# Linear attention: the reciprocals of the denominators spread by one matmul a group instead of two

## The chip, the cores and the metric

The kernel runs on one core of one Trainium2 chip. The metric is the device time of one execution in microseconds (us); lower is better. Engines are named as in the profile: PE is TensorE's matmul and PEld its weight load, DVE is VectorE, ACT is ScalarE, POOL is GpSimd, and SP is SyncE, whose queue issues most of the transfers.

## The reference, cut to what matters

The reference is a decoder layer over x of 2 x 2048 x 512 values in f32: linear attention, then attention to 154 keys, then a mixture of experts. Only the first part matters here:

```python
q_proj = _elu1(einsum('bhnd,hdf->bhnf', q, proj_matrix))   # 16 heads, 128 features
k_proj = _elu1(einsum('bhnd,hdf->bhnf', k, proj_matrix))
kv   = einsum('bhnf,bhnd->bhfd', k_proj, v)
attn = einsum('bhnf,bhfd->bhnd', q_proj, kv)
z    = 1.0 / (einsum('bhnf,bhf->bhn', q_proj, k_proj.sum(axis=2)) + 1e-08)
x    = x + (attn * z[..., None]) heads side by side @ w_out + b_out
```

Each token has one denominator for each of 16 heads, and each of the 32 values of a head is multiplied by the reciprocal of that one denominator.

## The kernel before

Four stages follow one another, each in a block that all engines enter together: `project` (queries, keys, values, and the sums over the keys), `attend_linear`, `attend_cross` and `experts`. The change touches the first two.

Where more precision is wanted than PE's fp32r format keeps, a number is held in two parts: HI, the value rounded to fp32r, and LO, the rest. A product takes several matmuls over these parts.

In `project`, `ks_out(b)` (L552) puts the sums of the keys of one batch into `ks_w`. It has one matrix of 128 x 32 for each head. It is zero but for one column, the number of the head's group, g. Four copies on DVE of 128 x 4 values do that for 16 heads.

`attend_linear` works on 8 blocks of 512 tokens. The 16 heads stand in G = 4 groups of 4; head j of a group has partitions 32j to 32j+31. In `attend_group` (L1176, L1182) the matmuls with `ks_w` add up over the groups into `p_den`: row 32j+g is the denominator of head j of group g. ACT copies the bank to `den[:, 0]` and adds 1e-8 (L960), DVE takes the reciprocal in two halves of 256 columns (L1049), ACT rounds each half to HI (L965), POOL subtracts it to get LO (L924), and PE spreads: for each group a 0/1 matrix `spread[:, g]` copies row 32j+g to the 32 rows of head j, once for HI and once for LO, into one PSUM bank (`spread_out`, L1191). DVE multiplies the numerators by that bank (`normalise`, L1054). ACT and POOL split the product for the output projection (L971, L936).

Every engine runs through the same 8 slots for a block, and in each slot PE works on three blocks: heads of the block ahead, projection and layer norm of this one, and the queries XQ of the next attention for the one behind:

```python
    2: [("R", 0), ("R", 1), ("R", 2), ("R", 3), ("XQ", 2, 0, 12)],
    3: [("ND", 0), ("O", 0, 0, 12)],
```

R is `spread_out`, XQ is `queries` (L1226, 12 matmuls), O is `out_proj` (L1204), T is the transposes (L1213), ND is `attend_group`. Slot 0 holds XQ 0 and slot 1 XQ 1 of the block behind. R, XQ, O and T share three PSUM banks in the order in which they come, so each waits until the job three before it was read: in slot 2, R 2 waits for the read of XQ 1, R 3 for that of R 0, and XQ 2 for that of R 1. DVE reads them in its own order: in slot 2 it is `query(i-1, 1)` (L1091), `normalise` 0, a head (L1086), `normalise` 1 and 2, a head, `normalise` 3. The first query needs ACT's half of it before (L989).

The constants come in three DMAs on SP's queue, counted by `const_in`: `spread`, `bq` and `bias`. One for `x` follows.

Of the kernel before, what the change touches and what calls it, by code (L numbers as in the profile page):

```python
# [18 lines left out]
F32 = mybir.dt.float32  # L19
# [3 lines left out]
ACT = mybir.ActivationFunctionType  # L23
AX = mybir.AxisListType

P = 128
# [6 lines left out]
H = 16  # L33
# [41 lines left out]
def constants():  # L75

    ident = np.eye(P, dtype=np.float32)
    quad = np.arange(P) // HD
    key = np.arange(P) % HD
    mask = (quad[:, None] == np.arange(HG)).astype(np.float32)  # L80
    mask_keys = mask * (key < KREM)[:, None]

    spread = np.zeros((P, G, P), np.float32)
    for g in range(G):
        for p in range(P):
            spread[32 * quad[p] + g, g, p] = 1

    pick = (np.arange(P)[:, None] % HD == np.arange(E)).astype(np.float32)
    lower = np.zeros((P, E, E), np.float32)
    for e in range(E):  # L90
        lower[:, e, :e] = 1
    small = np.concatenate([mask, mask_keys], 1)
    return {
        "ident": ident, "small": small, "spread": spread.reshape(P, -1), "lower": lower.reshape(P, -1), "pick": pick,
    }


# [92 lines left out]
def project(nc, a, NBLK, BLK, x_blk, q_dram, ident, f_w, k3, q_in, q_out, kv_w, ks_w, w_kv, first_heads, half,  # L190
# [81 lines left out]
    with ExitStack() as ctx:  # L272
# [36 lines left out]
        def bank_of(key):  # L309
            return pj[POS[key] % BANKS]  # L310
# [18 lines left out]
        with nc.Block() as block:  # L329
# [169 lines left out]
            def _(dve):  # L499
# [46 lines left out]
                def ks_out(b):  # L546
                    if b == 0:
                        dve.wait_ge(zero_set, 2)
                    dve.wait_ge(filled, POS[(b, "KS")] + 1)
                    flat = ks_w[:, b].rearrange("p h d -> p (h d)")  # L550
                    for j in range(HG):
                        last = nc.vector.tensor_copy(flat[:, j * HD:(H - HG + j) * HD + G:HG * HD + 1],  # L552
                                                     bank_of((b, "KS"))[:, 2 * j:2 * (H - HG + j) + 1:2 * HG])
                        last.then_inc(*((dve_read, 1) if j == HG - 1 else (sums_set, 1)))

                def bend(key):

# [205 lines left out]
def attend_linear(nc, a, NBLK, BLK, x_blk, q_dram, x1_dram, xq_dram, ident, f_w, q3, q_in, q_out, xq_out, kv_w, ks_w, qp,  # L763
# [35 lines left out]
    with ExitStack() as ctx:  # L799
# [10 lines left out]
        u_ln = sb("u_ln", [P, 2, C, TB], F32R)  # L810
        spread = sb("spread", [P, G, P], F32R)
        rec = sb("rec", [P, 2, TB], F32R)
        bias = sb("bias", [P, D])
        x = sb("x", [P, TT, D])
        xn = sb("xn", [P, 2, D])
# [2 lines left out]

        bq = sb("bq", [P, C])
        tiny = sb("tiny", [P, 1])  # L820
        stats = sb("stats", [P, TT, 6])
        mv = sb("mv", [P, TT, 2])
        rstd = sb("rstd", [P, TT])
# [37 lines left out]
        with nc.Block() as block:  # L861
            @block.sync
            def _(sp):
                def load_q(b, g):

                    sp.wait_ge(h_full, H * (b - 2) + HG * (g + 1))
                    if b == NBLK - 1 and g == 0:
                        for landed in q_out:
                            sp.wait_ge(landed, 16 * Q_DMAS * NBLK)
                    load_group(sp, q_dram, b, g, q3, q_in[g])  # L870

                def query_out(m, g):
                    sp.wait_ge(xq_taken, G * m + g + 1)
                    sp.dma_start(xq_dram[m].rearrange("s p n -> p s n")[:, :, g * TB:(g + 1) * TB],
                                 xq[:, g % 2].bitcast(F32)).then_inc(xq_out[g % 2], 16)

                sp.dma_start(spread_raw.rearrange("p g n -> p (g n)"), a["spread"]).then_inc(const_in, 16)
                sp.dma_start(bq[:], a["bqT"]).then_inc(const_in, 16)
                sp.dma_start(bias[:], a["b_out"].broadcast_to([P, D])).then_inc(const_in, 16)
                sp.dma_start(x[:], x_blk[0]).then_inc(x_in, 16)  # L880

                def slot(i, s, ahead, now, behind):
                    if behind and s in (1, 2, 3, 7):
                        query_out(i - 1, (1, 2, 3, 7).index(s))
                    if i >= 0 and i + 2 < NBLK and s in (2, 4, 6, 7):
                        load_q(i + 2, (2, 4, 6, 7).index(s))
                    if now and s == 6:
                        sp.wait_ge(o_taken, TT * (i + 1))
                        sp.dma_start(x1_dram[i], x[:].rearrange("p t d -> p (t d)")).then_inc(x1_out, 16)
                    if now and s == 7 and i + 1 < NBLK:  # L890
                        sp.wait_ge(x1_out, 16 * (i + 1))
                        sp.wait_ge(xn_set, TT * (i + 1))
                        sp.dma_start(x[:], x_blk[i + 1]).then_inc(x_in, 16)
                    if i == NBLK - 1 and s == 0:

                        sp.wait_ge(h_full, H * (NBLK - 1))
                        sp.dma_start(first.ctx[:], a["ctxT"][0].rearrange("(c p) n -> p c n", p=P))\
                            .then_inc(first.sems["ctx_in"], 16)
                        sp.dma_start(first.bk[:], a["bkT"]).then_inc(first.sems["ctx_in"], 16)
                    if i == 0 and s == 7:  # L900
                        sp.wait_ge(wo_lo, 1)
                        sp.wait_ge(wq_lo, 1)
                        for n, name in enumerate(("WkT", "WvT", "WoT")):
                            sp.dma_start(staged(stage, n), a[name].rearrange("(c p) n -> p c n", p=P)).then_inc(next_in, 16)

                turns(slot)
                sp.wait_ge(next_in, 48)
                sp.wait_ge(scaled, 1)
                sp.wait_ge(x1_out, 16 * NBLK)

            @block.gpsimd
            def _(pool):
                nc.gpsimd.memset(tiny[:], 1e-8).then_inc(tiny_set, 1)
                pool.wait_ge(tiny_set, 1)
                pool.wait_ge(const_in, 48)
                def add_bias(i, t):
                    if t == 0:
                        pool.wait_ge(x_in, 16 * (i + 1))
                    nc.gpsimd.tensor_tensor(x[:, t], x[:, t], bias[:], ALU.add).then_inc(xb_set, 1)

                def reciprocal_low(i, n):
                    cols = slice(n * TB // 2, (n + 1) * TB // 2)
                    pool.wait_ge(rec_hi, 2 * i + n + 1)
                    nc.gpsimd.tensor_tensor(rec[:, LO, cols], den[:, 1, cols], rec[:, HI, cols].bitcast(F32),  # L924
                                            ALU.subtract).then_inc(rec_set, 1)

                for i in range(NBLK):
                    if i == 0:
                        pool.wait_ge(spread_set, 1)
                    reciprocal_low(i, 0)  # L930
                    reciprocal_low(i, 1)
                    add_bias(i, 0)
                    add_bias(i, 1)
                    for g in range(G):
                        pool.wait_ge(norm_hi, G * i + g + 1)
                        nc.gpsimd.tensor_tensor(u_att[:, LO, g], num[:, g], u_att[:, HI, g].bitcast(F32), ALU.subtract)\  # L936
                            .then_inc(norm_lo, 1)
                    add_bias(i, 2)
                    add_bias(i, 3)
                    for t in range(TT):  # L940
                        pool.wait_ge(aggr_set, 2 * (TT * i + t + 1))
                        nc.gpsimd.tensor_tensor(rstd[:, t:t + 1], mv[:, t, 1:2], half[:, 0:1], ALU.pow)\
                            .then_inc(rstd_set, 1)

            @block.scalar
            def _(act):
# [15 lines left out]
                def reciprocal_high(i, n):  # L962
                    cols = slice(n * TB // 2, (n + 1) * TB // 2)
                    act.wait_ge(recip_set, 2 * i + n + 1)
                    nc.scalar.copy(rec[:, HI, cols], den[:, 1, cols]).then_inc(rec_hi, 1)  # L965

                def normalised(i, g):
                    if g == 0:
# [13 lines left out]

                def query(m, g):
                    if m == 0 and g == 0:
                        act.wait_ge(const_in, 48)
                    if m or g >= 2:
                        act.wait_ge(xq_out[g % 2], 16 * (2 * m + g // 2))
                    act.wait_ge(xq_full, G * m + g + 1)
# [56 lines left out]
            def _(dve):  # L1045
# [49 lines left out]
                def slot(i, s, ahead, now, behind):  # L1095
                    first, second = [(lambda h=h: head(i + 1, h)) if ahead else (lambda: None)
                                     for h in range(PER * s, PER * (s + 1))]
                    if i == -1 and s == SLOTS - 1:
                        dve.wait_ge(const_in, 48)
                        nc.vector.tensor_copy(spread[:], spread_raw).then_inc(spread_set, 1)  # L1100
                    if s == 1 and now:
                        reciprocal(i, 1)
# [50 lines left out]
            def _(pe):  # L1153
# [32 lines left out]
                def spread_out(i, g):  # L1186
                    bank_free((i, "R", g))
                    if g == 0:
                        pe.wait_ge(rec_set, 2 * (i + 1))
                    for s in (HI, LO):  # L1190
                        mm = nc.tensor.matmul(bank_of(i, "R", g)[:], spread[:, g], rec[:, s], start=(s == HI),  # L1191
                                              stop=(s == LO))
                    mm.then_inc(r_full, 1)

                def out_proj(i, t, lo, hi):
                    if lo == 0:
# [1481 lines left out]
```

## Time and profile before

| | |
|---|---|
| median of 3 runs | 2379.21 us (2376.5 to 2381.13) |
| the profiled execution | 2380.94 us, of which the span of the instructions is 2379.2 us |
| mean granted clock of TensorE | 0.983 of full speed |
| linear stage | about 417 to 743 us of the span |
| PE busy, whole span | 2278.0 us (96%) |

The page gives sums over all stages. Whether a matmul less is worth its time is to be read from the stage it stands in: there the timeline tells what PE waits for, right behind that matmul.

### The profile page before, as it was taken

The page shows a single profiled execution, that of the slowest core. Times are in us where ns is not written, and L with a number is a line of the kernel's source. Part 1 is how long each engine was busy: PE and PEld are TensorE (multiplying, and loading weights), DVE is VectorE, ACT ScalarE, POOL GpSimd, SP SyncE. Part 2 cuts the span into 40 slices and gives each one's busy share as a digit, 9 for nine tenths or more (in the row PEclk, how much of TensorE's full clock was granted, in tenths as well). Part 3 has the DMA queues.
Part 4 walks back from the last instruction along what each step waited for, and adds up shares of the span by engine and source line. Part 5 has one row for each costly group of instructions (what it writes and reads, how often), then busy time and mean ns, then how long its engine had stood idle before and what let it go on. Part 6 is the DMA issues. An engine that isn't in the chain of part 4 may idle for free.

```text
span 2379.2 us, 34267 instructions
## 1 busy us (share of the span) xinstructions
PE 2278.0 (96%) x12200; PEld 1775.7 (75%) x12200; DVE 1390.5 (58%) x2258; ACT 1158.5 (49%) x2745; POOL 838.9 (35%) x820
## 2 busy tenths in 40 slices
PE   7999999899998899998799999999999999999998
PEld 6888886566666566665588878888788887888887
DVE  5555456777774668777644466444664445644444
ACT  3555566767663767774544444333343333433332
POOL 1444345333341245545677762111111111111111
PEclk9999999999999899999899999999999999999999
DMA  7655546666646457784656546454345543464442
GB/s 209 161 146 128 134 107 157 210 187 195 177 142 181 102 145 188 185 225 138 217 174 212 177 141 214 171 177 142 129 153 201 177 142 125 136 215 139 140 139 77
DMA packets 140218, 387.46 MB, mean 163 GB/s; under 512 B 15920, under 2 KB 38064, under 8 KB 123440
## 3 DMA queue, kind: packets, MB, share of 16 engines
q1 hardware_dynamic: 139760, 384.77, 53.9%
q8 instruction: 98, 1.61, 0.3%
q10 hardware_dynamic: 288, 0.49, 0.1%
q14 instruction: 72, 0.59, 0.1%
HBM read 254.00 MB, written 104.07 MB: 151 GB/s over the span
## 4 chain that ended last, share of the span: by engine, by line
PE 51%; DVE 1%; issue 0%; ACT 0%; DVEq 0%
PE ex_pg L2593 32%; PE ex_pd L2609 18%; DVE ex_xb L2410 0%; PE ex_pd L2559 0%; PE ex_pd L2570 0%; DVE ex_up L2430 0%; DVE ex_acc L2447 0%; ACT ex_xb L2260 0%; DVE stage L2406 0%; DVE ex_ht L2439 0%; DVE ex_lg L2348 0%; DVE ex_rank L2382 0%; DVE ex_gt L2379 0%; DVE ex_rank L2380 0%; DVE ex_g L2423 0%
## 5 line engine op out<-in xcount | busy, mean ns | idle before, releaser
L2593 PE MATMUL ex_pg<-ex_xb,first_wg 128*128 128x512 f32 x3360 | 821.5, 391 | 12.0 <-DVE ex_up L2430 7.0
L2593 PEld LDWEIGHTS ex_pg<-ex_xb,first_wg 128*128 128x128 f32 x3360 | 632.0, 189 | 153.0 <-issue 15.7
L2609 PE MATMUL ex_pd<-ex_wd,ex_ht 128*128 128x512 f32 x1920 | 486.4, 389 | 2.9 <-issue 2.6
L2609 PEld LDWEIGHTS ex_pd<-ex_wd,ex_ht 128*128 128x128 f32 x1920 | 360.0, 188 | 79.1 <-issue 4.5
L2447 DVE SCALAR_TENSOR_TENSOR ex_acc<-ex_pd,ex_share,ex_acc 128x512 f32<-128x512 f32 x320 | 239.7, 749 | 302.4 <-PE ex_pd L2609 302.2
L2267 ACT COPY ex_m<-ex_pg 128x512 f32<-128x512 f32 x240 | 141.1, 588 | 383.5 <-PE ex_pg L2593 383.4
L2211 POOL TENSOR_TENSOR ex_h<-ex_g,ex_up 128x512 f32<-128x512 f32 x80 | 103.3, 1292 | 553.3 <-issue 458.2
L1590 ACT ACTIVATE cr_prob<-cr_s_bank,cr_top 128x154 f32<-128x154 f32 x512 | 194.7, 401 | 89.3 <-DVE cr_top L1700 86.6
L422 POOL TENSOR_TENSOR pr_ks_sum<-pr_ks_sum,pr_kp 128x512 f32<-128x512 f32 x128 | 165.2, 1291 | 161.6 <-DVE pr_kp L570 150.0
L2271 ACT ACTIVATE ex_g<-ex_g 128x512 f32<-128x512 f32 x160 | 101.3, 633 | 238.0 <-DVE ex_g L2423 165.5
L2203 POOL TENSOR_TENSOR ex_wd<-stage,ex_wd 128x512 fp32r<-128x512 f32 x80 | 105.8, 1343 | 260.1 <-ACT ex_wd L2248 260.1
L2278 ACT CAST ex_ht<-ex_h 128x512 fp32r<-128x512 f32 x160 | 99.4, 622 | 133.1 <-POOL ex_h L2211 133.0
L570 DVE SCALAR_TENSOR_TENSOR pr_kp<-pr_pk,pr_kp 128x512 f32<-128x512 f32 x128 | 88.5, 691 | 104.1 <-ACT pr_kp L475 103.4
L1700 DVE TENSOR_REDUCE cr_top<-cr_s_bank 128x3 f32<-128x462 f32 x192 | 110.4, 578 | 59.3 <-PE cr_s_bank L1865 59.2
L1865 PEld LDWEIGHTS cr_s_bank<-cr_k_w,cr_q 96*128 96x128 f32 x512 | 74.1, 199 | 77.1 <-issue 37.2
L2416 DVE TENSOR_TENSOR ex_g<-ex_pg,ex_m 128x512 f32<-128x512 f32 x80 | 55.3, 691 | 130.1 <-PE ex_pg L2593 124.9
L2439 DVE TENSOR_TENSOR ex_ht<-ex_h,ex_ht 128x512 fp32r<-128x512 f32 x160 | 122.2, 764 | 0.1
L1865 PE MATMUL cr_s_bank<-cr_k_w,cr_q 96*128 96x154 f32 x512 | 98.5, 302 | 20.1 <-DMA cr_q<-xq_scratch 11.9
L1590 ACT ACTIVATION_READ_ACCUMULATOR cr_prob<-cr_s_bank,cr_top 128x1 f32 x512 | 110.1, 215 | 0.0
L1927 PE MATMUL cr_bank<-cr_wo,cr_u 128*128 128x512 f32 x384 | 103.4, 407 | 4.0 <-DVE cr_x L1729 4.0
L1086 DVE SCALAR_TENSOR_TENSOR qp<-li_h_bank,qp 128x512 f32<-128x512 f32 x112 | 75.2, 681 | 46.7 <-ACT qp L1006 46.0
L473 ACT ACTIVATE pr_kp<-pr_pk 128x512 f32<-128x512 f32 x124 | 73.2, 590 | 52.8 <-PE pr_pk L702 52.8
(222 smaller groups left out, 3588.9 us busy)
## 6 DMA issues: line engine op xcount, KB each, us to landing
first_wg<-w_scratch SPq DMA_DIRECT2D x60, 1024.0 KB, 5.1
first_wg<-w_scratch SPq DMA_DIRECT2D x60, 768.0 KB, 4.3
w_scratch<-first_wg SPq DMA_DIRECT2D x20, 1792.0 KB, 6.8
stage<-in_units SPq DMA_DIRECT2D x60, 512.0 KB, 6.9
qk<-pr_kq SPq DMA_DIRECT2D x192, 128.0 KB, 2.4
qk<-q_scratch SPq DMA_DIRECT2D x96, 256.0 KB, 4.7
cr_q<-xq_scratch SPq DMA_DIRECT2D x96, 256.0 KB, 8.0
q_scratch<-pr_kq SPq DMA_DIRECT2D x128, 128.0 KB, 2.3
```

The source lines that it names most:

```text
L422: nc.gpsimd.tensor_tensor(part, part, slot(step), ALU.add).then_inc(ks_step, 1)
L1590: last = nc.scalar.activation(prob[:, n % 2, t, j, 0:KEYS], s_bank[(MU * n + v) % SBANKS][:, at * KEYS:(at + 1) * KEYS], ACT.Exp, bias=top ...
L1700: nc.vector.tensor_reduce(dst.rearrange("p t j -> p (t j)") if t == t_end else dst[:, :, 0], src, AX.X, ALU.max, negate=True).then_inc(top ...
L1865: mm = nc.tensor.matmul(s_bank[at % SBANKS][:, k * KEYS:(k + 1) * KEYS], q3[:, n % QRING, j, t * P:(t + 1) * P], k_w[:, n // G // BLK, j, ...
L1927: mm = nc.tensor.matmul(bank_of("O", m)[:], u[:, s, g, tile_cols(m)], wo[:, w, g], start=(n == 0), stop=(n == 3 * G - 1))
L2203: nc.gpsimd.tensor_tensor(wd[:, n % 2, LO, cols], d_raw[:, cols], wd[:, n % 2, HI, cols].bitcast(F32), ALU.subtract).then_inc(wd_lo, 1)
L2211: nc.gpsimd.tensor_tensor(h[:, f, 1], g[:, f, 1], up[:], ALU.mult).then_inc(h1_set, 1)
L2267: nc.scalar.copy(dst[:], pg[f][BANK[j]][:]).then_inc(m_set, 1)
L2439: nc.vector.tensor_tensor(ht[:, LO, f, k], h[:, f, k], ht[:, HI, f, k].bitcast(F32), ALU.subtract)\
L2447: nc.vector.scalar_tensor_tensor(acc[:, at], bank_of("D", n, i)[:], share[:, NT * half + at, e:e + 1], acc[:, at], ALU.mult, ALU.add).then ...
L2593: mm = nc.tensor.matmul(pg[f][BANK[j]][:], wg[:, f, j, s, c * P:(c + 1) * P], xb[:, j, m, c * TB:(c + 1) * TB], start=(k == 0 and j in FRESH),
L2609: mm = nc.tensor.matmul(bank_of("D", n, i)[:], ht[:, s, f, k, t * P:(t + 1) * P], wd[:, n % 2, m, f * D:(f + 1) * D], start=(at == 0), sto ...
```

## The change

Each denominator is made in two rows of `p_den`, 32j+g and 32j+4+g, by a second column in `ks_w`. After the reciprocal, ACT multiplies by a column `low_rows`, 1 in rows 4 to 31 of each 32 and 0 in rows 0 to 3, and rounds: `rec_low` is zero in the first four rows and the rounded value in the others. POOL's subtraction, written rounded, then leaves the rounded value in the first row and the rest in the second: `rec_both`. `spread` has ones in both rows, so one matmul a group adds both parts. `ks_out` makes 8 copies for a batch instead of 4, one small constant is loaded more, and the waits on `const_in` count it. POOL also waits until the spreading of the block before has read `rec_both`.

```diff
@@ constants() @@
-            spread[32 * quad[p] + g, g, p] = 1
+            spread[HD * quad[p] + g, g, p] = 1
+            spread[HD * quad[p] + G + g, g, p] = 1
+    low_rows = (np.arange(P) % HD >= G).astype(np.float32)[:, None]
@@ project(), VectorE, ks_out(b) @@
                     for j in range(HG):
-                        last = nc.vector.tensor_copy(flat[:, j * HD:(H - HG + j) * HD + G:HG * HD + 1],
-                                                     bank_of((b, "KS"))[:, 2 * j:2 * (H - HG + j) + 1:2 * HG])
-                        last.then_inc(*((dve_read, 1) if j == HG - 1 else (sums_set, 1)))
+                        for again in range(2):
+                            first = j * HD + again * G
+                            last = nc.vector.tensor_copy(flat[:, first:first + (G - 1) * (HG * HD + 1) + 1:HG * HD + 1],
+                                                         bank_of((b, "KS"))[:, 2 * j:2 * (H - HG + j) + 1:2 * HG])
+                            last.then_inc(*((dve_read, 1) if again and j == HG - 1 else (sums_set, 1)))
@@ attend_linear() @@
         rec = sb("rec", [P, 2, TB], F32R)
+        rec_low, rec_both = rec[:, 0], rec[:, 1]
+        low_rows = sb("low_rows", [P, 1])
@@ SyncE @@
                 sp.dma_start(bq[:], a["bqT"]).then_inc(const_in, 16)
+                sp.dma_start(low_rows[:], a["low_rows"]).then_inc(const_in, 16)
                 sp.dma_start(bias[:], a["b_out"].broadcast_to([P, D])).then_inc(const_in, 16)
@@ GpSimd @@
-                pool.wait_ge(const_in, 48)
+                pool.wait_ge(const_in, 64)
-                def reciprocal_low(i, n):
+                def both_parts(i, n):
                     cols = slice(n * TB // 2, (n + 1) * TB // 2)
                     pool.wait_ge(rec_hi, 2 * i + n + 1)
-                    nc.gpsimd.tensor_tensor(rec[:, LO, cols], den[:, 1, cols], rec[:, HI, cols].bitcast(F32),
+                    if i:
+                        pool.wait_ge(r_full, G * i)
+                    nc.gpsimd.tensor_tensor(rec_both[:, cols], den[:, 1, cols], rec_low[:, cols].bitcast(F32),
                                             ALU.subtract).then_inc(rec_set, 1)
@@ ScalarE @@
                     act.wait_ge(recip_set, 2 * i + n + 1)
-                    nc.scalar.copy(rec[:, HI, cols], den[:, 1, cols]).then_inc(rec_hi, 1)
+                    if i == 0:
+                        act.wait_ge(const_in, 64)
+                    nc.scalar.activation(rec_low[:, cols], den[:, 1, cols], ACT.Copy, scale=low_rows[:]).then_inc(rec_hi, 1)
@@ ScalarE query, VectorE slot: act.wait_ge / dve.wait_ge(const_in, 48) become (const_in, 64) @@
@@ TensorE, spread_out(i, g) @@
-                    for s in (HI, LO):
-                        mm = nc.tensor.matmul(bank_of(i, "R", g)[:], spread[:, g], rec[:, s], start=(s == HI),
-                                              stop=(s == LO))
-                    mm.then_inc(r_full, 1)
+                    nc.tensor.matmul(bank_of(i, "R", g)[:], spread[:, g], rec_both, start=True, stop=True).then_inc(r_full, 1)
```

## Rows read from the trace of the kernel before

**Rows 1.** The page, part 1: busy time of each engine over the whole execution.

```profile
PE 2278.0 (96%) x12200; PEld 1775.7 (75%) x12200; DVE 1390.5 (58%) x2258; ACT 1158.5 (49%) x2745; POOL 838.9 (35%) x820
```

**Rows 2.** Stretch view: length, then PE, PEld, DVE, ACT, POOL busy, clock, DMA.

```profile
465.00:700.00 235.00, 228.28 (x1191) 150.29 (x1190) 177.59 (x323) 167.14 (x301) 85.30 (x84) 1.00 0.63 187
```

**Rows 3.** Tile view of rec: the spreading matmuls; ns min/median/max, first and last start.

```profile
L1191 PE MATMUL li_bank<-li_rec,li_spread x64: 387/397/792, 432.1 to 707.4; 128*128 128x512 f32 x64
```

**Rows 4.** Waits of PE, 462 to 700 us: us in total, times, longest.

```profile
PE li_bank L1226 <- DVE li_num L1054: 2.8, 6, 0.5
```

**Rows 5.** Timeline of block 1's reciprocals and spreading; start us, us, engine, [idle before].

```profile
465.33 2.93 PE L1226 MATMUL li_bank<-li_u_ln,wq 128*128 128x512 f32 x12
...
466.87 0.39 ACT L965 CAST li_rec<-li_den 128x256 fp32r<-128x256 f32 x1
...
468.32 0.67 ACT L989 ACTIVATE li_xq<-li_bank,li_bq 128x512 fp32r<-128x512 f32 x1
...
468.56 1.09 PE L1191 MATMUL li_bank<-li_rec,li_spread 128*128 128x512 f32 x4
...
469.06 0.74 DVE L1091 SCALAR_TENSOR_TENSOR li_xq<-li_bank,li_bq,li_xq 128x512 fp32r<-128x512 f32 x1
...
469.71 0.68 DVE L1054 TENSOR_TENSOR li_num<-li_num,li_bank 128x512 f32<-128x512 f32 x1
...
469.85 1.32 PE L1191 MATMUL li_bank<-li_rec,li_spread 128*128 128x512 f32 x4 [0.20 <-DVE li_xq L1091]
...
470.91 1.28 DVE L1054 TENSOR_TENSOR li_num<-li_num,li_bank 128x512 f32<-128x512 f32 x2
...
471.64 3.02 PE L1226 MATMUL li_bank<-li_u_ln,wq 128*128 128x512 f32 x12 [0.47 <-DVE li_num L1054]
```

**Rows 6.** Timeline of the last block, weight load of its XQ 2.

```profile
707.70 2.63 PEld L1226 LDWEIGHTS li_bank<-li_u_ln,wq 128*128 128x128 f32 x12 [0.30 <-DVE li_num L1054]
```

**Rows 7.** Timeline of block 0's spreading.

```profile
432.13 3.78 PE L1191 MATMUL li_bank<-li_rec,li_spread 128*128 128x512 f32 x8
...
432.46 0.69 DVE L1086 SCALAR_TENSOR_TENSOR qp<-li_h_bank,qp 128x512 f32<-128x512 f32 x1 [1.09 <-ACT qp L1006]
...
433.45 0.69 DVE L1054 TENSOR_TENSOR li_num<-li_num,li_bank 128x512 f32<-128x512 f32 x1 [0.30 <-PE li_bank L1191]
```

**Rows 8.** Groups of ACT by form, 425 to 745 us: busy us, mean ns.

```profile
L951 ACT COPY li_num<-li_p_num 128x512 f32<-128x512 f32 x30 | 17.1, 570 | 1.4 <-PE li_p_num L1182 1.4
...
L960 ACT ACTIVATE li_den<-li_p_den,li_tiny 128x512 f32<-128x512 f32 x8 | 5.4, 675 | 0.9 <-PE li_p_den L1176 0.9
```

**Rows 9.** Timeline, three places: end of the first stage, and behind the first batch's copies.

```profile
265.10 0.69 DVE L532 TENSOR_TENSOR pr_kq<-pr_pj,pr_kq 128x512 fp32r<-128x512 f32 x1 [4.13 <-ACT pr_kq L450]
...
412.96 3.65 SPq L342 DMA_DIRECT2D q_scratch<-pr_kq  x8
...
414.84 0.36 DVE L552 COPY ks_w<-pr_pj 128x4 f32<-128x4 f32 x4
```

**Rows 10.** Timeline of the linear stage's start: constants in, first denominators out.

```profile
417.51 0.44 SPq L878 DMA_DIRECT2D li_bq<-in_bqT  x1
...
425.10 0.43 DVE L1100 CAST li_spread<-li_den 128x512 fp32r<-128x512 f32 x1 [3.79 <-DMA li_bias<-in_b_out]
...
426.16 0.69 ACT L960 ACTIVATE li_den<-li_p_den,li_tiny 128x512 f32<-128x512 f32 x1
```

**Rows 11.** Stretch view, columns as in rows 2; the seventh is the granted clock.

```profile
427.50:431.10 3.60, 0.50 (x2) 0.19 (x1) 3.60 (x4) 2.73 (x6) 0.73 (x1) 1.00 0.75 178
431.10:437.90 6.80, 6.47 (x19) 3.82 (x23) 4.64 (x8) 5.99 (x12) 5.81 (x6) 0.50 0.16 34
468.50:471.70 3.20, 2.53 (x10) 1.24 (x9) 3.20 (x6) 3.14 (x6) 2.08 (x2) 1.00 1.05 386
726.60:729.80 3.20, 1.31 (x8) 0.86 (x9) 2.90 (x5) 1.17 (x2) 0.00 (x0) 1.00 0.43 164
...
786.08:789.49 3.41, 1.81 (x17) 1.50 (x20) 3.41 (x4) 2.17 (x11) 0.00 (x0) 1.00 0.00 0
```

More of the change, by code:

```diff
@@ L93, in constants @@
     return {
-        "ident": ident, "small": small, "spread": spread.reshape(P, -1), "lower": lower.reshape(P, -1), "pick": pick,
+        "ident": ident, "small": small, "spread": spread.reshape(P, -1), "low_rows": low_rows, "lower": lower.reshape(P, -1), "pick": pick,
     }
@@ L929, in _ @@
                         pool.wait_ge(spread_set, 1)
-                    reciprocal_low(i, 0)
-                    reciprocal_low(i, 1)
+                    both_parts(i, 0)
+                    both_parts(i, 1)
                     add_bias(i, 0)
@@ L984, in query @@
                     if m == 0 and g == 0:
-                        act.wait_ge(const_in, 48)
+                        act.wait_ge(const_in, 64)
                     if m or g >= 2:
@@ L1098, in slot @@
                     if i == -1 and s == SLOTS - 1:
-                        dve.wait_ge(const_in, 48)
+                        dve.wait_ge(const_in, 64)
                         nc.vector.tensor_copy(spread[:], spread_raw).then_inc(spread_set, 1)
```

## The prediction

> **What bounds the kernel now.** I began with the page's busy times: PE works in 96% of the span [rows 1], so a matmul taken away could be worth its full time. This sum is over four stages, and 64 of 12200 matmuls are touched, all in the linear stage between 432 and 707 us [rows 3]. So I read the stretch view next: from 465 to 700 us, where the blocks repeat, PE is busy 228.28 of 235 us and DVE 177.59 [rows 2]. PE is the bound of the stage as a whole. The idle 6.7 us are few, but where they lie decides. The waits of PE show it: in this stretch XQ 2 waits six times for `normalise`, 2.8 us together [rows 4]. That is once in each block, and XQ 2 is the job that stands right behind the four spreadings. PE is not the bound at the place where its work is taken away.
>
> The timeline of one block shows who is [rows 5]. Read it from XQ 1: its 12 matmuls start at 465.33 and run to 468.26. ACT takes the bank at 468.32 until 468.99. DVE then has four things one behind the other: `query` at 469.06, `normalise` 0 at 469.71, a head, and `normalise` 1 at 470.91. The row of `normalise` 1 and 2 lasts 1.28 us for two, so the first is done near 471.6, and XQ 2 starts at 471.64. On the other side, R 0 and R 1 (four matmuls) start at 468.56 and are over at 469.65, before DVE begins `normalise` 0 at 469.71. R 2 waits to 469.85 for DVE's read of XQ 1. So the chain that sets XQ 2 is XQ 1, ACT, DVE. The spreading hangs beside it and is never late for it.
>
> **The change, part by part.** *The matmuls.* 32 of 64 go. The mean of one is 397 ns [rows 3], but matmuls overlap. The price is from start to start: 12 of XQ take 2.93 us, about 0.23 us each [rows 5]. For a block that is 4 x 0.23 = 0.92 us of PE's queue. In blocks 1 to 6 it comes free between R 0 and XQ 2, where PE then waits longer for the same DVE instruction: R 0 and R 1 are ready earlier and DVE, which is still busy with its query, takes them at the same time. R 2 stays bound to the read of XQ 1, R 3 to that of R 0, XQ 2 to that of R 1. Gain 0. The cover is DVE's chain; without it the gain would be 0.92 us a block. In block 7 there is no head ahead, and DVE is quicker, but XQ 2's weight load still waits for `normalise` [rows 6]: gain 0 too.
>
> Block 0 is different. There is no XQ behind it, and the clock is at its lower level, 0.50, from 431.1 to 437.9 us [rows 11]: eight matmuls take 3.78 us [rows 7], 0.43 to 0.47 us each. Here DVE does wait for R 0, 0.30 us, until 433.45 [rows 7]. With one matmul R 0 would be ready about 0.4 us sooner, at about 433.0. DVE then is held by its head, which starts at 432.46 and hands over about 0.6 us later (the pitch from 469.71 to 470.91 over two instructions, [rows 5]), at 433.06. So 0.4 us come free for DVE. PE gains 4 x 0.43 = 1.7 us, but its next heads wait for DVE's heads, and further on in this block DVE has no room: what is kept is DVE's 0.4, less the price below. Between 0.0 and 1.7 us; I take 0.4.
>
> *ACT's instruction* becomes an ACTIVATE with a scale read from a tile. The trace has no such row with a scale. The nearest pair takes the same 128x512 from PSUM: the plain copy 570 ns, the ACTIVATE with a column as bias 675 ns [rows 8]. So a column costs 0.10 us; below, 0 if the scale is read for nothing. I take 0.10. There are two of these a block. The first lies where ACT next waits for PE. The second starts at 466.87 in front of ACT's heads, and the query of XQ 1 follows on the same queue at 468.32, just when XQ 1 is over (468.26) [rows 5]. ACT has no slack there, so 0.10 us goes into the chain to XQ 2. Blocks 1 to 6: 0.6 us. Block 7: the heads are gone and ACT waits for PE, 0. Block 0: the second half is what the first spreading waits for, 0.1 us, so the 0.4 above becomes 0.3.
>
> *POOL's subtraction* keeps its shape. Its new wait, for the spreading of the block before, was met some 30 us earlier; what is queued behind it (bias additions, the LO halves of the product) does not move. The added rows in `ks_w` leave the shape of the 256 denominator matmuls as it is: nothing.
>
> *The copies in `ks_out`.* Four take 0.36 us together [rows 9], so four more about 0.3 us. In the first batch DVE's next instruction waits 4.13 us for ACT [rows 9]. In the second they stand at the end of the first stage: the copies start at 414.84, one large copy follows, and DVE would be done at about 416.1 instead of 415.8. SP still issues its stores until 412.96 + 3.65 = 416.61 [rows 9], and all engines enter the next stage together. Hidden, with 0.5 us of slack; without that cover, 0.3 us.
>
> *The DMA of `low_rows`* is issued before those of `bias` and `x`. An issue takes 0.44 us [rows 10], so `bias` comes up to 0.44 us later, and DVE's cast of `spread`, which waits for it, starts at 425.54 instead of 425.10 and ends at 425.97. ACT's first denominators need it at 426.16 [rows 10]. Slack 0.19 us: 0. If the small transfer itself were slow and landed 1.5 us late, it would cost 1.3 us once; that is my upper bound.
>
> *The sum:* 0.6 - 0.3 = +0.3 us, bounds -1.7 (block 0 gives all, the column costs nothing) and about +2.2 (0.7 for the column, nothing from block 0, 1.3 for the DMA, 0.2 rounding). The profiled execution had 2380.94 us (span 2379.2), so 2381.2 on its scale. It lies 1.7 us above the median of the runs, 2379.21; on the median's scale the forecast is 2379.5 us, with a range of its own from 2377 to 2382. I call no change what is within 0.2%, 4.8 us, about what a measurement of this kernel can tell.
>
> **Rival 1, PE's time counts in full: faster.** If the stage were PE-bound at the spreading too, as 228 of 235 us busy suggest [rows 2], 28 matmuls x 0.23 + 4 x 0.43 = 8.2 us would go: 2371.0. Against it stand PE's waits in every block [rows 4, 6]. It holds only if DVE's chain is itself drawn forward by the spreading, for which I see no link. Chance 0.05.
>
> **Rival 2, TensorE's clock falls in the new gaps: slower.** PE is busy 2.53 of the 3.2 us around a spreading [rows 11]. The change takes away 0.92, which leaves about 1.6, half. What the trace shows at either side: before the fall at 431.1, PE was busy 0.50 of 3.6 us; with 1.31 of 3.2 us between 726.6 and 729.8 the clock kept 1.00; but in the cross stage 1.81 of 3.41 us, with short matmuls, stood before a fall at 789.5 [rows 11]. The busy share alone does not tell, and the spreading's matmuls are long ones. A fall costs what follows: the one at 431.1 lasted 6.8 us, at half speed 3.4 us lost; with no gap left in what follows it may last half as long, 1.7 us. It decides from two or three blocks on: three falls give 5 to 10 us, 2385 to 2389. The Trainium skill speaks for this rival ("TensorE: Matmul & The Clock Gate", section "A second HAM failure mode: psum-queue depth-cycling"): PE that idles for a moment between groups of matmuls, waiting for PSUM banks, can swing between the two clocks, and loses throughput although each matmul looks as before. Today's spreading has such waits in each block and the clock stays at 1.00 there, so no run here shows it at this place yet. Chance that some falls come 0.18, that they cost over 4.8 us 0.12.
>
> **Rival 3, the gain is there but paid out later:** the 0.92 us could reach the end of a block if XQ 2 were let start by something else than `normalise` 1. The order of the banks excludes it. In block 0 PE's 1.7 us might be kept whole, 2377.8. That is inside no change; chance 0.06, taken into the first case.
>
> **How the numbers follow.** My forecast with its neighbours inside 0.2%: 0.82. Faster: 0.05 for rival 1 and 0.01 for the rest. Slower: 0.12, nearly all rival 2. The runs before spread by 4.6 us themselves, and clock falls in the cross stage may shift by a few us. The range goes to 2376.5 below, near the lowest run, which leaves out rival 1, and to 2384.5 above, which takes in the bound of the unknown costs and one or two falls.
>
> **What the profile would show.** Right: L1191 with 32 matmuls; PE's wait of XQ 2 for `normalise` grows from about 0.5 to about 1.0 us a block or more, and XQ 2 starts as long behind XQ 1 as now, 6.3 us from start to start, plus 0.1; ACT's L965 at about 0.50 us instead of 0.40; the clock at 1.00 from 465 to 700 us; the block's period unchanged. Wrong: a shorter period means that DVE's chain was not the bound; falls of the clock behind a spreading mean rival 2; a later first denominator means the DMA.

## The result, and the profile after

The changed kernel is slower. Its median is 2391.77 us (4 runs, 2389.2 to 2392.65), that of the kernel before in the same session 2378.52 us (4 runs, 2376.5 to 2381.13). The ratio is 1.005, with a 95% interval of 1.0038 to 1.0062. The forecast was 2379.5 us, with a range up to 2384.5.

The profiled execution took 2389.2 us with a span of 2387.4 us, 8.2 us more than the span before. It is the lowest of the four, and the profiled one of before, with 2380.94 us, stands near the top of its runs, so these two traces show less than the difference of the medians.

First the stretch view of the changed kernel, from the first fall of the granted clock in the repeating part to the last, cut where that clock (the sixth column behind the length, just before the DMA share) changes:

```profile
473.00:476.40 3.40, 3.40 (x9) 2.64 (x10) 1.59 (x3) 1.67 (x4) 3.32 (x3) 0.55 1.08 372
476.40:514.00 37.60, 35.81 (x188) 23.14 (x186) 27.79 (x52) 26.50 (x48) 10.85 (x12) 1.00 0.66 192
514.00:517.40 3.40, 3.33 (x8) 2.62 (x9) 1.80 (x4) 1.88 (x4) 3.11 (x3) 0.54 1.08 266
517.40:555.00 37.60, 35.99 (x189) 23.29 (x187) 28.83 (x52) 26.24 (x48) 11.07 (x12) 1.00 0.58 170
555.00:558.40 3.40, 3.06 (x7) 2.48 (x8) 2.08 (x4) 2.16 (x4) 2.83 (x3) 0.54 1.07 269
558.40:735.80 177.40, 166.88 (x860) 111.90 (x858) 127.50 (x240) 110.89 (x198) 64.21 (x64) 1.00 0.52 160
735.80:739.30 3.50, 3.10 (x7) 2.48 (x8) 0.26 (x1) 0.00 (x0) 0.00 (x0) 0.55 0.00 0
```

There are four short stretches at the lower clock level, 1.2 instead of 2.4 GHz, where the kernel before has none. Three of them begin within 0.4 us of the start of XQ 2 in blocks 1 to 3, behind a spreading. The fourth, at 735.8, does not: it stands in the last block, behind transposes, where PE's three waits are the same in the kernel before (0.94, 0.40 and 1.49 us). The timeline of block 1 answers to rows 5:

```profile
467.98 0.49 ACT L977 ACTIVATE li_rec<-li_den,li_low_rows 128x256 fp32r<-128x256 f32 x1
...
469.53 0.67 ACT L1001 ACTIVATE li_xq<-li_bank,li_bq 128x512 fp32r<-128x512 f32 x1
...
469.68 0.63 PE L1202 MATMUL li_bank<-li_rec,li_spread 128*128 128x512 f32 x2
...
471.06 1.09 PE L1202 MATMUL li_bank<-li_rec,li_spread 128*128 128x512 f32 x2 [0.75 <-DVE li_xq L1103]
...
472.12 1.28 DVE L1066 TENSOR_TENSOR li_num<-li_num,li_bank 128x512 f32<-128x512 f32 x2
...
472.85 4.61 PE L1235 MATMUL li_bank<-li_u_ln,wq 128*128 128x512 f32 x12 [0.70 <-DVE li_num L1066]
```

As forecast, the removed matmuls leave idle time. PE waits 0.75 us for the read of XQ 1 instead of 0.20, and 0.70 for `normalise` 1 instead of 0.47. The forecast had put all of it in front of XQ 2 (1.0 us or more); the larger part came in front of R 2. XQ 1 started at 466.44, so XQ 2 starts 6.41 us behind it; before it was 6.31 [rows 5]. The new thing is the last row. The 12 matmuls of XQ 2 take 4.61 us where they took 3.02. That is 1.6 us lost; in block 3 it is 4.56 us, 1.5 lost.

The tile views of the two kernels give the length of the repeating part, from the start of ACT's first XQ instruction to that of its last:

| | first | last | length | low stretches in it |
|---|---|---|---|---|
| before | 465.1 | 741.1 | 276.0 us | 0 |
| after | 466.2 | 749.0 | 282.8 us | 4 |

The 8.2 us split as follows. 1.0 stands ahead of the linear stage, which starts at 418.07 instead of 417.09: among the first matmuls of the kernel, where nothing was changed, four transposes took 1.11 us instead of 0.66. 0.1 lies between the start and the first XQ, 6.8 in the repeating part, and 0.3 behind it.

### The profile page after: what moved, and what is told of

The parts are those of the page before. It is cut to its first block, busy times and chain, and to the rows that moved or that the text cites. A ratio compares the mean times of both kernels' runs of the same rounds, so it can differ in the third digit from the quotient of the medians.

```text
span 2387.4 us, 34228 instructions
## 1 busy us (share of the span) xinstructions
PE 2276.9 (95%) x12168; PEld 1774.1 (74%) x12168; DVE 1390.2 (58%) x2266; ACT 1159.1 (49%) x2745; POOL 838.3 (35%) x820
## 4 chain that ended last, share of the span: by engine, by line
PE 50%; DVE 1%; issue 0%; ACT 0%; DVEq 0%
PE ex_pg L2602 32%; PE ex_pd L2618 18%; DVE ex_xb L2419 0%; PE ex_pd L2568 0%; DVE ex_up L2439 0%; PE ex_pd L2579 0%; DVE ex_acc L2456 0%; ACT ex_xb L2269 0%; DVE stage L2415 0%; DVE ex_ht L2448 0%; DVE ex_lg L2357 0%; DVE ex_rank L2391 0%; DVE ex_gt L2388 0%; DVE ex_rank L2389 0%; DVE ex_g L2432 0%
## 5 line engine op out<-in xcount | busy, mean ns | idle before, releaser
L1235 PE MATMUL li_bank<-li_u_ln,wq 128*128 128x512 f32 x384 | 100.6, 415 | 5.8 <-DVE li_num L1066 4.2
```

## The experiments

Theory A is rival 2 of the prediction: the clock falls in the gap that the missing matmuls leave. Theory B is that other parts of the change lengthen the chain. "Length" is the same measure as above. The lengths in what follows come from one profiled execution of each kernel, the ratios from all runs, against the kernel before as it ran beside them.

**e1: the matmuls back, all else as changed.**

```diff
-nc.tensor.matmul(bank_of(i, "R", g)[:], spread[:, g], rec_both, start=True, stop=True).then_inc(r_full, 1)
+for again in range(2):
+    mm = nc.tensor.matmul(bank_of(i, "R", g)[:], spread[:, g], rec_both, start=True, stop=True)
+mm.then_inc(r_full, 1)
```

> The changed kernel, but each spreading matmul is issued twice into its bank (the second writes the same values again), so PE has as many spreading matmuls as before, and all other parts of the change stay. Theory A (the clock falls in the gap that the missing matmuls leave): no low stretch behind a spreading, the four of the changed kernel at 473.0, 514.0, 555.0 and 735.8 us are gone, and the time is that of before plus about 0.6 us for ACT's dearer instruction: 2378 to 2381 us. Theory B (the dearer ACT instruction, the extra copies, the extra transfer or the extra wait lengthen the chain): as the changed kernel, 2389 to 2393 us.

Measured: 2379.95 us (12 runs), ratio to before 1.0004 (0.9996 to 1.0013). With 32 useless matmuls more, the kernel is 12 us faster than the changed one. Two rows of its timeline show the gap closed; PE's wait is 0.46 us, and XQ 2 takes 3.01 us again:

```profile
471.54 1.32 PE L1203 MATMUL li_bank<-li_rec,li_spread 128*128 128x512 f32 x4 [0.29 <-DVE li_xq L1103]
473.33 3.01 PE L1237 MATMUL li_bank<-li_u_ln,wq 128*128 128x512 f32 x12 [0.46 <-DVE li_num L1066]
```

No fall behind a spreading is left. One low stretch is, at 732.7 us, behind the transposes of the last block. So theory A was wrong about the fourth fall of the changed kernel, which stands at the same place: it comes with the spreading matmuls present too, and is not shown to be an effect of their removal. Length 278.1 us (466.7 to 744.8), 2.1 more than before; with 1.6 taken for that fall, 0.5 is left for ACT.

**e2: only the matmuls taken away.** It spreads the reciprocal's rounded part alone and leaves the rest out, so its results are less exact.

```diff
-for s in (HI, LO):
-    mm = nc.tensor.matmul(bank_of(i, "R", g)[:], spread[:, g], rec[:, s], start=(s == HI), stop=(s == LO))
+mm = nc.tensor.matmul(bank_of(i, "R", g)[:], spread[:, g], rec[:, HI], start=True, stop=True)
```

> The kernel before with one part of the change alone: only the HI matmul of each spreading is issued, the one with the rest is left out, so the reciprocals are spread as rounded to fp32r. POOL still computes the rest. Theory A: 32 matmuls less are enough, clock falls behind some of the spreadings and a time of 2385 to 2393 us. Theory B: no slower than before, 2371 to 2379 us.

Measured: 2390.4 us (6 runs), ratio 1.005 (1.0037 to 1.0064), the same ratio as the whole change. In this execution the clock fell behind the spreading in each of the seven blocks 1 to 7. The first, second and last of them in the stretch view, with what lies between the first two:

```profile
472.00:475.30 3.30, 3.30 (x9) 2.52 (x9) 0.97 (x2) 1.05 (x2) 3.30 (x4) 0.51 1.09 354
475.30:513.00 37.70, 35.92 (x189) 23.29 (x188) 28.53 (x53) 27.03 (x50) 10.72 (x12) 1.00 0.65 193
513.00:516.30 3.30, 3.30 (x9) 2.58 (x8) 1.08 (x2) 1.18 (x3) 3.30 (x3) 0.52 1.00 237
...
717.80:721.10 3.30, 3.30 (x9) 2.58 (x8) 0.00 (x0) 0.65 (x2) 3.30 (x4) 0.52 0.00 0
```

Length 286.5 us (464.7 to 751.2), 10.5 more than before: 1.5 us for each of seven.

**e3: only ACT's dearer instruction.** The column of ones, `one_col`, is set once by POOL at the start of the stage; those lines are left out here.

```diff
-nc.scalar.copy(rec[:, HI, cols], den[:, 1, cols]).then_inc(rec_hi, 1)
+nc.scalar.activation(rec[:, HI, cols], den[:, 1, cols], ACT.Copy, scale=one_col[:]).then_inc(rec_hi, 1)
```

> The kernel before with ACT's rounding done as in the changed kernel, an ACTIVATE with its scale read from a column (of ones): the dearer instruction alone. The column adds 0.10 us to each. Theory A: plus 0.6 us over the six blocks in which it lies in the chain, 2378 to 2381 us, no new low stretch. Theory B: several us slower, 2385 to 2392 us.

Measured: 2379.56 us (12 runs), ratio 1.0004 (0.9994 to 1.0014). Length 276.4 us (465.7 to 742.1), 0.4 more than before, with no fall in it. The groups of ACT by form, first of the kernel before, then of this one, then of the changed one, give the price of the column as 0.10 us (401 against 504 ns):

```profile
L965 ACT CAST li_rec<-li_den 128x256 fp32r<-128x256 f32 x16 | 6.4, 401 | 3.2 <-DVE li_den L1049 3.2
```

```profile
L967 ACT ACTIVATE li_rec<-li_den,li_one_col 128x256 fp32r<-128x256 f32 x16 | 8.1, 504 | 3.1 <-DVE li_den L1051 3.1
```

```profile
L977 ACT ACTIVATE li_rec<-li_den,li_low_rows 128x256 fp32r<-128x256 f32 x16 | 8.1, 504 | 3.1 <-DVE li_den L1061 3.1
```

**e4 and e5: the gap shortened from DVE's side.** In slot 2 DVE does `normalise` 1 ahead of the head, in e4 in the changed kernel, in e5 in the kernel before.

```diff
                         normalise(i, 0)
+                        normalise(i, 1)
                     first()
...
-                        normalise(i, 1)
                         normalise(i, 2)
```

> The changed kernel with DVE's order in slot 2 changed: normalise 1 comes before the head instead of behind it, so that XQ 2 can start about 0.6 us earlier in blocks 1 to 6 and the gap behind the spreading is that much shorter. Theory A: the pace of the blocks is set there, so 6 x 0.6 = 3.6 us come free, and with the shorter gap some or all of the falls are gone: 2374 to 2386 us, 2375 if no fall is left. Theory B: 3.6 us at most, 2387 to 2389 us.

> The kernel before with DVE's new order of slot 2 alone (normalise 1 ahead of the head). Theory A: XQ 2 starts up to 0.6 us earlier in six blocks, but PE's own eight spreading matmuls now end almost as late, so about 0.5 us a block: 2376 to 2378 us, and no low stretch behind a spreading. If the order of DVE and not the closed gap had saved the last kernel but one, this one would gain as much over before as that one gained over the changed kernel, 12 us: 2367.

e4: 2379.48 us (12 runs), ratio 1.0 (0.999 to 1.0011). Length 272.8 us (466.1 to 738.9), no fall. That is inside the range of theory A, but not the 2375 it gave for a kernel without a fall. e5: 2375.75 us (11 runs) against 2378.85 for before in its session, ratio 0.9986 (0.9977 to 0.9995). Length 272.4 us (464.5 to 736.9), no fall. That is far from the 2367 it would have reached if the order itself were worth 12 us. The timeline of PE in the two, e4 first:

```profile
470.90 1.09 PE L1202 MATMUL li_bank<-li_rec,li_spread 128*128 128x512 f32 x2 [0.76 <-DVE li_xq L1103]
472.09 3.04 PE L1235 MATMUL li_bank<-li_u_ln,wq 128*128 128x512 f32 x12
```

```profile
469.20 1.33 PE L1191 MATMUL li_bank<-li_rec,li_spread 128*128 128x512 f32 x4 [0.20 <-DVE li_xq L1091]
470.39 3.02 PE L1226 MATMUL li_bank<-li_u_ln,wq 128*128 128x512 f32 x12
```

In both the wait for `normalise` is gone. R 2 and R 3 start 1.19 us ahead of XQ 2 in both, whether they are two matmuls or four, since both are timed by DVE. By the lengths, the new order brings 3.6 us in the kernel before (276.0 to 272.4), by DVE's chain. In the changed kernel it brings 10.0 (282.8 to 272.8), because it takes the falls away besides. The medians fall by 3 and 12 us.

**e6 and e7: XQ 2 ahead of R 2 and R 3, a miss.**

```diff
-        2: [("R", 0), ("R", 1), ("R", 2), ("R", 3), ("XQ", 2, 0, 12)],
+        2: [("R", 0), ("R", 1), ("XQ", 2, 0, 12), ("R", 2), ("R", 3)],
```

> The changed kernel with PE's slot 2 in another order: R 0, R 1, XQ 2, R 2, R 3. The bank that XQ 2 takes is then that of XQ 1, free when DVE has read XQ 1, about 1.8 us before normalise 1 is done; R 2 and R 3 follow behind it and wait for nothing. Theory A: the gap shrinks to about 0.8 us, no fall in blocks 1 to 6, and now the removed matmuls count: XQ 2, R 2 and R 3 together end about 1.3 us earlier than in the kernel before, 6 x 1.3 less 0.6 for ACT: 2371 to 2374 us. Theory B: the order matters only by the wait, and the chain stays dearer: 2380 or more.

> The kernel before with the same order of PE's slot 2. Theory A: PE then is the bound there, so its four more matmuls count in full, 0.9 us a block more than in the changed kernel with this order: about 2374 to 2376 us, that is 5 to 6 us less than before, and 2 to 5 us more than the changed kernel in this order. Theory B: the change is worth nothing or less in this order too, 2374 or below and not slower than its counterpart.

Measured: e6, in the changed kernel, 2415.58 us (4 runs), ratio 1.0152 (1.0136 to 1.0168). e7, in the kernel before, 2403.06 us (4 runs), ratio 1.0096 (1.0082 to 1.011). I had followed the three banks up to XQ 2 and not one job further. With R 2 and R 3 behind XQ 2, O 0 is the third job after it and takes its bank, which DVE reads only a slot later. PE's waits in e6 (two rows), then in e7:

```profile
PE li_bank L1213 <- DVE li_xq L1103: 20.3, 6, 4.0
PE li_bank L1235 <- DVE li_xq L1103: 4.5, 6, 0.8
```

```profile
PE li_bank L1204 <- DVE li_xq L1091: 18.7, 6, 3.5
```

The gap in front of O 0, 3.0 to 4.0 us, is a second trial of theory A. In e6 it is longer than in e7 (3.99 and 3.48 us in block 1), and low stretches of 6.8 us begin near its end in each of blocks 1 to 6, two of which are:

```profile
479.10:485.90 6.80, 6.20 (x15) 4.90 (x16) 1.14 (x2) 0.97 (x3) 0.54 (x1) 0.50 0.71 194
523.50:530.30 6.80, 6.21 (x15) 4.87 (x16) 2.35 (x3) 0.97 (x3) 1.26 (x2) 0.50 0.71 193
```

e7 has such a stretch in blocks 1 and 2 only, and shorter ones of 3.4 us at that place in blocks 5 and 7. The changed kernel is again the slower, by 12.5 us in the medians, where the expectation had it 2 to 5 us faster. The lengths are 310.8 us (465.1 to 775.9) in e6 and 302.6 (465.8 to 768.4) in e7, so 8.2 of the difference lie in this stage.

**e8 and e9: R 0, R 1, R 2, XQ 2, R 3.** Now O 0 takes the bank of R 2.

```diff
-        2: [("R", 0), ("R", 1), ("R", 2), ("R", 3), ("XQ", 2, 0, 12)],
+        2: [("R", 0), ("R", 1), ("R", 2), ("XQ", 2, 0, 12), ("R", 3)],
```

> The changed kernel with PE's slot 2 in the order R 0, R 1, R 2, XQ 2, R 3. XQ 2 takes the bank of R 0, free when normalise 0 is done, 1.2 us before normalise 1; O 0 takes the bank of R 2 and O 1 that of XQ 2, whose read on DVE should just be over by then. Theory A: PE's gap between R 1 and XQ 2 shrinks from 2.6 to about 1.4 us with R 2 in it, no or few falls in blocks 1 to 6, and XQ 2 is 1.2 us earlier in each of them, less the 0.6 for ACT: 2371 to 2376 us. If O 1 waits for DVE's read of XQ 2, part of that is given back. Theory B (a slower chain whatever PE does): 2380 or more.

> The kernel before with the same order. XQ 2 can start at about 470.5 instead of 471.6, right behind R 2, and R 3 costs its 0.46 us behind it: 0.7 us a block, 4 us over six blocks, 2374 to 2377 us. Theory A says that here, where PE does not wait for DVE, the changed kernel's shorter spreading shows for the first time as time saved or at least as no loss: this kernel is not faster than its counterpart.

Measured: e8, in the changed kernel, 2379.13 us (12 runs), ratio 0.9994 (0.9985 to 1.0004), a miss. e9, in the kernel before, 2374.57 us (12 runs) against 2379.29, ratio 0.998 (0.9971 to 0.999), inside its range and the fastest kernel of the study. But theory A had said that e9 would not be faster than e8, and it is, by 4.6 us: the second miss. PE's waits in e9, 462 to 715 us, no longer hold XQ 2:

```profile
PE li_bank L1191 <- DVE li_xq L1091: 2.1, 7, 0.7
PE li_h_bank L1166 <- DVE qp L1086: 1.1, 5, 0.2
PE li_p_den L1176 <- DVE qp L1086: 1.0, 1, 1.0
PE li_bank L1204 <- POOL li_u_att L936: 0.8, 1, 0.8
```

The length is 272.2 us (467.8 to 740.0) in e9 with no fall, and 273.0 us (466.6 to 739.6) in e8 with one at 726.7, behind the transposes of the last block. Take 1.6 off for that fall and e8's stage would be 0.8 us shorter than e9's: an estimate from one execution of each that the removed matmuls show as time, but a small one.

The spans of the two profiled executions differ by 9.5 us, far more than these lengths. The difference lies behind the linear stage, between the last XQ instruction and the first matmul of the experts, where no kernel of this study changes anything. This stretch in e8, then in e9:

```profile
739.60:1140.00 400.40, 355.89 (x2321) 249.70 (x2321) 279.55 (x552) 265.90 (x1153) 174.30 (x194) 0.94 0.66 168
740.00:1130.90 390.90, 349.27 (x2320) 246.68 (x2320) 281.07 (x552) 265.68 (x1153) 174.48 (x194) 0.96 0.68 172
```

The same code takes 400.4 us at a mean granted clock of 0.94 and 390.9 at 0.96. In the kernel before it takes 397.7, in the changed one 397.9, in e6 400.6 and in e7 392.5. So this stretch moves by up to 10 us from one profiled execution to another. Whether it is longer behind the changed kernel as a rule, or only in these executions, no run shows.

**e11: the changed kernel once more.**

> The changed kernel unaltered, profiled once more on another execution. Its first profiled execution had four low stretches in the linear stage and the lowest of four times, 2389.2 us; the others took 2391 to 2393. Theory A: the falls come at the same places of the block, but their number differs between executions, 3 to 7, and the linear stage is about 1.6 us longer for each. Theory B: the linear stage has the same length whatever the number of low stretches.

Measured: 2390.33 us, before beside it 2377.59, one run each. Six low stretches lie in the repeating part: behind the spreadings of blocks 1 to 4, and two in the last block, one behind its spreading and one behind its transposes. Length 285.5 us (466.6 to 752.1).

The lengths put side by side, beside the number of falls in them: 276.0 with none, 282.8 with four, 285.5 with six, 286.5 with seven (e2, without ACT's dearer instruction). Of these falls three, five and seven stand behind a spreading. Less 0.4 us for ACT in the second and third, a fall costs 1.6, 1.5 and 1.5 us.

## Why the prediction was wrong, point by point

- **The chain beside the spreading.** Right. XQ 2 starts 6.41 us behind XQ 1, was 6.31, and the wait for `normalise` 1 grew, though to 0.70 us and not to 1.0, as the rest of the idle time came in front of R 2. No part of the 0.92 us a block came back.
- **"Gain 0. The cover is DVE's chain"** is the step that failed, together with the "clock at 1.00 from 465 to 700 us" that it rests on. The time of the removed work was priced at nothing, rightly. But the idle time that it leaves was priced at nothing too, and it cost 1.5 to 1.6 us each time the clock fell behind it. Removing the matmuls alone (e2) gives the whole ratio of 1.005; putting them back (e1) brings the ratio to 1.0004.
- **Rival 2** is what happened, and I had given it 0.18, with 0.12 for more than 4.8 us. Its price was well estimated (1.7 us for a short fall, measured 1.5 to 1.6). The number was not: I took three and the traces show four, six and seven in the linear stage. Three short falls make 5 us, seven make 10.5. The evidence that misled me most was a single row: the clock kept 1.00 with PE busy 1.31 of 3.2 us at 726.6 [rows 11]. At the same place of the last block, with 1.31 of 3.40 us, it did fall in the changed kernel, and also in e1, where all matmuls are back:

```profile
732.40:735.80 3.40, 1.31 (x8) 0.83 (x8) 3.23 (x6) 1.72 (x4) 0.00 (x0) 1.00 0.45 171
```

  So a gap that kept the clock in one execution is no proof that it is safe.
- **The Trainium skill**, as cited there ("TensorE: Matmul & The Clock Gate", section "A second HAM failure mode: psum-queue depth-cycling"), says that PE idling for moments between groups of matmuls, as it cycles through PSUM banks, can make the clock swing between its two levels, so that throughput is lost while the median matmul looks as before. The trace agrees: the waits are for banks, and the median of the 384 XQ matmuls is 393 ns against 389. It also shows the loss in single matmuls: the longest of the 384 takes 792 ns, was 506.
- **ACT's column.** Right: 0.10 us an instruction, 0.4 us in all (e3) where I had 0.6.
- **Block 0.** I took a gain of 0.3 us; from the stage's start to the first XQ there are 48.1 us instead of 48.0. Nothing of it is left there; its further way I did not follow. The first denominator comes 9.23 us behind the start of the stage, was 9.07. The prediction had named that as a sign of a late transfer, but it is none: a copy of ACT in front of it (L961), which waits for PE, is already as much late (5.71 instead of 5.55).
- **The copies, the transfer, POOL's wait.** Right, as far as can be told: e1 holds all of them, its median is within the noise of before, and its length leaves 0.1 us beside ACT and one fall. In the changed kernel the cast of `spread` started at 425.24, before the first denominators at 427.30.
- **Rival 1** is excluded by the waits. **Rival 3**: in another order (e8) the removed matmuls may show, as less than 1 us.

Open is which blocks fall. In the changed kernel's first profile blocks 4 and 5 have the same waits as block 3 and keep the clock. Here are XQ 2 of block 3 and of block 4:

```profile
555.34 4.56 PE L1235 MATMUL li_bank<-li_u_ln,wq 128*128 128x512 f32 x12 [0.69 <-DVE li_num L1066]
...
596.51 3.02 PE L1235 MATMUL li_bank<-li_u_ln,wq 128*128 128x512 f32 x12 [0.69 <-DVE li_num L1066]
```

The stretches ahead of them, of blocks 1 and 3, which fell, and of block 4, which did not; the last two start equally far, 0.56 us, ahead of the spreading:

```profile
469.60:473.00 3.40, 1.85 (x7) 0.74 (x6) 3.34 (x6) 3.34 (x8) 2.18 (x2) 1.00 1.05 387
...
551.60:555.00 3.40, 2.19 (x8) 1.00 (x6) 3.20 (x6) 3.34 (x7) 2.66 (x3) 1.00 0.59 218
592.78:596.18 3.40, 2.19 (x8) 0.99 (x6) 3.20 (x6) 3.34 (x7) 2.65 (x3) 1.00 0.59 211
```

PE did the same work in both, and in the second execution (e11) block 4 fell too, with the same waits. So the size of the gap does not decide alone; the moment at which it comes may count beside it. No run tried that. A block without a fall lasts 39.6 us (the heads ahead of the spreading start at 592.87 and at 632.46), and with one it lasts 41.2 to 41.3 us (469.21, 510.42, 551.69), so each fall also moves the next gap.

Nor is it shown why the median of the changed kernel lies 13 us above that of before, when the lengths with six and seven falls are 9.5 and 10.5 us more. More falls in the executions that were not profiled, and the stretch behind the linear stage, which varies by 10 us, can each make up the rest.

## What to carry to other kernels

Idle time of TensorE can have a price of its own: before taking matmuls out of a place where PE then waits, see how much it idles there already and what runs at full speed right behind. If the gap grows, close it first (here by the order of DVE in e4 or of the jobs in e8), or leave the cheap matmuls in. Here leaving them in was better: with the same orders e5 and e9, which keep them, have medians 3.7 and 4.6 us lower than e4 and e8. And when a job is moved in a ring of banks, follow the ring to the job that takes its bank, as e6 and e7 show.

## What the runs showed of the hardware

In the changed kernel PE had been busy 1.85 and 2.19 of the 3.40 us ahead of two falls, and 2.19 of 3.40 us at the same place of block 4 without a fall. A low stretch of 3.4 us cost 1.5 to 1.6 us, close to the half of its length. In e6 stretches of 6.8 us came, behind gaps of which that in block 1 was 3.99 us long.
